# A graph network on one core: 448 late columns that carry their own row numbers, edge records loaded eight halves at a time, and one PSUM operand in each step of the sort

## The reference

```python
x = _layernorm(x + _L0_gnn_ref(x, edge_index, ...))   # mean of x[src] over dst, two matmuls, rows normalised
x = _layernorm(x + _L1_gnn_ref(x, edge_weight1, ...)) # one weight matrix per edge type, segment_sum over dst
x = _layernorm(x + _L2_gnn_ref(x, edge_index, ...))   # five rounds of: m = h @ W; agg = segment_sum(m[src], dst); GRU
x = _layernorm(x + _L3_gnn_ref(x, edge_index, ...))   # below
# _L3_gnn_ref, an MLP on every edge, summed over the edge's own source node:
row, col = edge_index[0], edge_index[1]
h = silu(concatenate([x[row], x[col], edge_attr]) @ eW1 + eb1)
m_ij = silu(h @ eW2 + eb2)
agg = segment_sum(m_ij, row)
update = silu(concatenate([x, agg]) @ nW1 + nb1) @ nW2 + nb2
```

## Time and profile before

| what | value |
|---|---|
| median of 3 runs | 10688.34 us |
| time of the profiled execution | 10691.69 us |
| its span in the profile | 10689.9 us, 154416 instructions |
| POOL busy | 8037.9 us (75%), 8249 instructions |
| PE, PEld busy | 6257.1 us (59%), 5701.5 us (53%) |
| DVE busy | 5456.2 us (51%) |
| ACT busy | 2205.1 us (21%) |
| first and last scatter of the sort start at | 75.8 and 1804.5 us |
| layer 0's gathers start at | 1815.5 us |
| layer 1's | 2933.7 us |
| layer 2's five rounds | 4044.8 us on |
| layer 3's | 9601.2 to 10652.7 us |

### The profile page before, as it was taken

The page is one execution under the profiler, slowest core; times in us unless marked ns, Lnnn a source line. Parts: engine busy times, 40 slices in busy tenths (PEclk is TensorE's granted clock), DMA queues, the critical chain, the costliest instruction groups (busy, mean ns, idle before and its releaser), DMA issues. The chain is left out here.

```text
span 10689.9 us, 154416 instructions
## 1 busy us (share of the span) xinstructions
PE 6257.1 (59%) x41996; PEld 5701.5 (53%) x41997; DVE 5456.2 (51%) x13690; ACT 2205.1 (21%) x6330; POOL 8037.9 (75%) x8249
## 2 busy tenths in 40 slices
PE   0000000555444436777677767776777688879998
PEld 0000000343333336777677767776777687878887
DVE  9993001444334434555455545554555466656666
ACT  1000000111133321111111111111111133336665
POOL 6777777777777777777777777777777777777776
PEclk9999999666655557888898878888989899989999
DMA  2000001222322233333433343334333433342223
GB/s 66 2 2 2 21 7 32 73 77 78 68 74 59 59 54 97 109 109 109 95 109 108 109 94 109 108 108 93 109 109 109 94 108 108 108 89 62 62 62 54
DMA packets 443301, 830.51 MB, mean 78 GB/s; under 512 B 179834, under 2 KB 260703, under 8 KB 442439
## 3 DMA queue, kind: packets, MB, share of 16 engines
q0 software_dynamic: 329728, 718.19, 26.8%
q1 hardware_dynamic: 113349, 109.89, 3.5%
HBM read 739.76 MB, written 87.77 MB: 77 GB/s over the span
## 5 line engine op out<-in xcount | busy, mean ns | idle before, releaser
L595 POOL DMA_INDIRECT rows<-state_table,rec x4160 | 4065.7, 977 | 1275.5 <-issue 1233.8
L666 DVE TENSOR_TENSOR agg<-agg,l_prod 128x250 f32 (+2 forms) x5824 | 2218.3, 381 | 3305.3 <-PE l_prod L643 1697.3
L643 PE MATMUL l_prod<-onehot,rows 128*128 128x125 f32 x16640 | 2538.4, 316 | 1234.3 <-DMA rows<-state_table,rec 656.9
L643 PEld LDWEIGHTS l_prod<-onehot,rows 128*128 128x128 f32 x16640 | 2359.8, 227 | 1377.3 <-DVE agg L666 1030.8
L640 PE MATMUL l_prod<-rows,onehot 128*125 128x130 f32 (+1 forms) x3328 | 758.8, 402 | 2100.4 <-DMA rows<-in_x_dram,rec 1569.0
L640 PEld LDWEIGHTS l_prod<-rows,onehot 128*125 128x125 f32 x3328 | 663.2, 296 | 2174.2 <-issue 1827.7
L294 POOL DMA_INDIRECT slots_table<-rec_stage,row_stage x784 | 809.4, 1032 | 305.8 <-issue 246.7
L649 DVE TENSOR_TENSOR onehot<-iota_row,rec 128x500 f32<-128x500 f32 x1465 | 987.1, 674 | 41.9 <-PEq L108 41.8
L1587 POOL DMA_INDIRECT l_gathered<-xcol_table,l_slots x832 | 799.2, 961 | 262.3 <-issue 253.0
L595 POOL DMA_INDIRECT rows<-in_x_dram,rec x832 | 800.0, 962 | 253.8 <-issue 250.2
L595 POOL DMA_INDIRECT rows<-rel_table,rec x832 | 793.4, 954 | 261.8 <-issue 228.6
(11 more groups left out here) (272 smaller groups left out, 8876.2 us busy)
## 6 DMA issues: line engine op xcount, KB each, us to landing
rows<-state_table,rec POOLq DMA_INDIRECT x4160
rel_table<-l_relrow SPq DMA_DIRECT2D x50, 500.0 KB
state_table<-l_row SPq DMA_DIRECT2D x200, 125.0 KB
slots_table<-rec_stage,row_stage POOLq DMA_INDIRECT x1312
rows<-in_x_dram,rec POOLq DMA_INDIRECT x832
rows<-rel_table,rec POOLq DMA_INDIRECT x832
l_gathered<-xcol_table,l_slots POOLq DMA_INDIRECT x832
slots_table<-fill SPq DMA_DIRECT2D x8, 936.0 KB
```

Source lines behind the costliest of these rows:

```text
L595: pool.indirect_dma_start(out=K["rows"][:, r, 0:width], out_offset=None, in_=table, in_offset=bass.IndirectOffsetOnAxis(ap=K["rec"][:, c, ...
L643: last = pe.matmul(p[:, s * SLOT:s * SLOT + LANES], K["rows"][:, r, s * D:(s + 1) * D], oh, start=True, stop=True)
L666: dve.tensor_tensor(into, into, of, ALU.add).then_inc(S.added, 1)
```

## The change

1. `LATE` is 448: the sort scatters 336 columns of key 1 in place of 528 (21 turns in place of 33), and the later phases scatter 66, 66, four times 66, and 52.
2. A late record has a 19th word, its row number (`REC_LATE`), in place of the separate `late_row`; the scatter takes its row number from the record.
3. `put_late` stands three turns before the end of the sort's scatters (`LAST_TURNS`).
4. In each step of the sort one operand lies in PSUM: the tile numbers (`tile_row`), the ones (`ones_c`), the running sums (`rank`) and the sum over five (`found`). The 128x2500 products stay as they were.
5. In layer 3 the records of eight halves, 288 KB, come with one DMA (`LOADED`), into one half of a ring of 16 (`DEEP`); gathered rows and one-hots keep 8 buffers (`FETCH`). The pipeline's loop unrolls 16 halves. SP's loop is written out.

```diff
-DEEP = 8
-FETCH = DEEP
+DEEP = 16
+FETCH = 8
+LOADED = 8
...
+REC_LATE = REC2 + 1
-LATE = 256
-LATE_LAYER, LATE_ROUND, LATE_LAST = 44, 34, 32
+LATE = 448
+LATE_LAYER, LATE_ROUND, LATE_LAST = 66, 66, 52
...
+        LAST_TURNS = 3
...
-        is_tile, rank = sb("is_tile", [L, FIVE, PART]), sb("rank", [L, FIVE, PART])
-        found, slot_i = sb("found", [L, PART]), sb("slot_i", [L, PART], I32)
+        is_tile, slot_i = sb("is_tile", [L, FIVE, PART]), sb("slot_i", [L, PART], I32)
-        ones_c = sb("ones_c", [L, PART])
...
+        rank = c.enter_context(nc.psum_tensor("rank", [128, 8, SLOT], F32))[0:L, 0:FIVE, 0:PART]
+        fixed = c.enter_context(nc.psum_tensor("fixed", [128, 4, SLOT], F32))
+        tile_row, ones_c, found = fixed[0:L, 0, :], fixed[0:L, 1, 0:PART], fixed[0:L, 2, 0:PART]
...
-                act.copy(K["late_row"][:], row[1][:, late]).then_inc(late_made, 1)
+                act.copy(late_all[:, :, REC2].bitcast(I32), row[1][:, late]).then_inc(late_made, 1)
...
-                for i in range(low, high):
-                    for h in range(2):
-                        stage(i, h, i + SC_TURNS, True)
-                if q == 1:
-                    put_late()
+                ends = [NOW_TURNS - LAST_TURNS, NOW_TURNS] if high == NOW_TURNS else [high]
+                for end in ends:
+                    for i in range(low, end):
+                        for h in range(2):
+                            stage(i, h, i + SC_TURNS, True)
+                    if end == NOW_TURNS - LAST_TURNS:
+                        put_late()
+                    low = end
...
+            step(dve.tensor_copy(tile_row, K["iota_row"][0:L, :]))
...
-                                               K["iota_row"][0:L, tiles][:, :, None].to_broadcast(part),
+                                               tile_row[:, tiles][:, :, None].to_broadcast(part),
...
-                out_offset=bass.IndirectOffsetOnAxis(ap=self.K["late_row"][:, self.at + c:self.at + c + 1], axis=0),
-                in_=self.K["late_rec"][:, c, :], in_offset=None).then_inc(self.done, 16)
+                out_offset=bass.IndirectOffsetOnAxis(ap=self.K["late_rec"][:, c, REC2:REC_LATE].bitcast(I32), axis=0),
+                in_=self.K["late_rec"][:, c, 0:REC2], in_offset=None).then_inc(self.done, 16)
...
+            def load(block):
+                area = block % (DEEP // LOADED)
+                if block >= DEEP // LOADED:
+                    sp.wait_ge(pre1_ok, block * LOADED - DEEP + LOADED)
+                sp.dma_start(slots[:, area * LOADED:(area + 1) * LOADED],
+                             table[:, block * LOADED * HALF:(block + 1) * LOADED * HALF, :]
+                             .rearrange("p (h k) w -> p h k w", k=HALF)).then_inc(slots_in[area], 16)
```

More of the change, by code:

```diff
@@ L385, in _ @@
             numbers = K["iota_row"][:, 0:TILES]
-            step(dve.memset(ones_c[:], 1.0))
+            step(dve.memset(ones_c, 1.0))
             dve.wait_ge(spares_made, 1)
@@ L605, in __init__ @@
         self.K, self.T, self.loaded, self.done = K, T, loaded, done
-        self.read, self.at = 0, 0
+        self.read = 0
     def load(self, sp, n):
@@ L612, in load @@
         sp.dma_start(self.K["late_rec"][:, 0:n, :].rearrange("p c w -> p (c w)"),
-                     self.T["late"][:, self.read * REC2:(self.read + n) * REC2]).then_inc(self.loaded, 16)
+                     self.T["late"][:, self.read * REC_LATE:(self.read + n) * REC_LATE]).then_inc(self.loaded, 16)
         self.read += n
@@ L1494, in edge_mlp @@
         loaded, zeroed = sem("loaded"), sem("zeroed")
-        slots_in = [sem(f"slots_in{q}") for q in range(DEEP)]
+        slots_in = [sem(f"slots_in{q}") for q in range(DEEP // LOADED)]
         onehot_ok = sem("onehot_ok")
@@ L1531, in _ @@
             STORE_LAG = NODE_LAG + 3
-            def load(i, off):
-                wait_half(sp, pre1_ok, i, off - DEEP)
-                sp.dma_start(slots[:, off % DEEP], table[:, bass.ds(number(i, off) * HALF, HALF), :])\
-                    .then_inc(slots_in[off % DEEP], 16)
+            def load(block):
[5 more added lines that the diff above has]
+                             .rearrange("p (h k) w -> p h k w", k=HALF)).then_inc(slots_in[area], 16)
             def store(k, buf):
@@ L1542, in store @@
                     .then_inc(stored[buf], 16)
-            def turn(i, off):
-                for q in range(DEEP):
-                    load(i, off + q)
-                    if q % 4 == 2:
-                        k = (off + q) // 4 - STORE_LAG
-                        if i is not None or k >= 0:
-                            store(k if i is None else i * (DEEP // 4) + k, k % 2)
             sp.wait_ge(late.done, 16 * LATE)
-            for j in range(DEEP):
-                load(None, j)
+            for block in range(DEEP // LOADED):
+                load(block)
             sp.wait_ge(zeroed, 1)
@@ L1568, in _ @@
             sp.dma_start(b2n[:], n_b2.rearrange("(a f) -> a f", a=1).to_broadcast([LANES, D])).then_inc(loaded, 16)
-            turn(None, DEEP)
-            turn(None, 2 * DEEP)
-            turn(None, 3 * DEEP)
-            with sp.Fori(4, HALVES // DEEP) as i:
-                turn(i, 0)
-            for k in range((HALVES // 4) - STORE_LAG, TILES):
+            for block in range(DEEP // LOADED, HALVES // LOADED):
+                load(block)
+                for k in range(block * LOADED // 4 - STORE_LAG, (block + 1) * LOADED // 4 - STORE_LAG):
+                    if k >= 0:
+                        store(k, k % 2)
+            for k in range(HALVES // 4 - STORE_LAG, TILES):
                 store(k, k % 2)
@@ L1582, in _ @@
                 q = half % FETCH
-                pool.wait_ge(slots_in[half % DEEP], half // DEEP * 16 + 16)
+                if half % LOADED == 0:
+                    pool.wait_ge(slots_in[half % DEEP // LOADED], half // DEEP * 16 + 16)
                 if half >= FETCH:
@@ L1732, in step @@
                     if i is not None:
-                        dve.wait_ge(stored[buf], i * 16 + (off // 4 - NODE_LAG - 1) // 2 * 16)
+                        dve.wait_ge(stored[buf], i * (DEEP // 8) * 16 + (off // 4 - NODE_LAG - 1) // 2 * 16)
                     elif k >= 2:
```

19 lines of the change are left out of this document (9 added, 10 removed).

## The result

The changed kernel takes 10655.5 us (median of 8 runs, 10651.35 to 10659.15), beside 10688.8 for the kernel before (8 runs, 10680.83 to 10698.51): ratio 0.997, 95% interval 0.996 to 0.9979. That is 33 us less, where the forecast was 42. The profiled execution took 10659.15 us, its span is 10657.4, 32.5 shorter than that of before.

The account below looks back on a forecast made before the run. The prediction took POOL's some 8200 indirect DMAs as the bound. Its terms, -44.7 + 2.5 - 2 + 1 + 0.9 = -42.3 us, took 10691.7 to 10649.4, by the median 10646; range 10632 to 10673.

Parts of the forecast that it names:

- Items 1 and 2: Sort steps: PSUM operands shorten first-key scatters, -44.7 us (bounds 0 and 58.6); DVE's own time +2.5 (0 to 10).
- the pointer operand of the earlier trace: Sort scans: pointer form took 349 ns with PSUM, 298 without; 50 scans by 0.05 us gave 2.5 us.
- Item 3: Sort and late groups: 192 scatters taken out save 245.0 us, put in cost 242.5; net -2 (-2.5 to +0.5).
- rival E: Phase tails: the moved scatters are free there, -242.5 us, 10404; chance 0.02.
- Item 4: Sort's end: the later, larger late table blocks scatters' landing; costs 3 us if caught, else 0; taken as +1.
- Item 5: Layer 3: POOL's first gather waits for 288 KB in place of 36, +0.9 us; later blocks are hidden.
- 8.5 us at a barrier: Barrier after a layer: listed among the small stretches left over besides POOL's DMAs; no change was forecast for it.
- B: Sort: an operand in PSUM frees nothing for a scatter; +2.4 us, 10691; chance 0.05.
- its half (scans): Sort: only the scans fail to free scatters, about 22 of the 44.7 us, 10668; chance 0.05.
- its "nothing": Sort: by the skill's rule that descriptor generation isn't contended, the PSUM operands would bring nothing; the prediction said the trace disagrees.
- C: First two sort parts: DVE slower with PSUM, 10 us before the first scatter, 10 before the 33rd; 10664; chance 0.06.
- D: Layer 3: POOL stops for blocks 24 times, 72 us at 3 us each, 10718; chance 0.06, including unnamed causes.

## Why the prediction was right, and by how much not

- **What bounds the kernel.** Right: every us of the change is on POOL, in the stretches named.
- **Items 1 and 2, the sort's operands.** Forecast -44.7 and +2.5, together -42.2; measured +0.9 and -43.3, together -42.4. The second key was to start at about 1090 and did at 1089.7, the mean was to be 975 and is 977. Part of this is luck: 2.5 us of DVE's own time were counted and 0.9 came. The six products keep 14.9 us with all else, where 13.9 were counted. DVE's share was 0.9 to the first scatter. Read over the two traces, the scan rose from 431 ns to 438 and the 128x560 comparison fell from 755 to 737: the pointer operand of the earlier trace rows, on which the 2.5 was built, has no part in it, and writing to PSUM costs 8 ns a reduction (1097 to 1105). Nor does the longer fixed cost of the Trainium skill ("VectorE: DVE Perf Modes", The TRN2 errata) show: as an estimate from its figures it came to 65 ns a step. The experiments show the operand as the cause scatter by scatter; the 42 us themselves only the first chip's two traces show.
- **Item 3, 192 scatters moved.** Forecast -2, measured -2.3. They are paid in full in the tails, as rows 6 had it (rival E is out).
- **Item 4, the late table.** Forecast +1, between 0 and 3; it is 0. ACT waited 3.4 us longer and the half ring covered it.
- **Item 5, layer 3's first block.** Forecast +0.9, measured 1.1 (from the drain's end to the first gather, 3.07 and 4.19 us).
- **The term that was missing.** The barriers were read once, as "8.5 us at a barrier", and taken as fixed. They are not: three of the four get 22, 22 and 20 more late scatters ahead of them (1.80, 1.80 and 1.63 us), and the sort ends 112 scatters behind a pause in place of 80 (2.51). That is 7.7 of the 9.8 us between 42.3 and 32.5. The rest is the 3.4 us over the gathers, which two executions can differ by, less about 1 us that item 4 didn't cost. It could have been read before: behind 44 late scatters the drain ends 6.93 us after the last, behind 32 it is 5.95.
- **The rivals.** B and its half (scans) are out on the first chip and in every timeline. So is the Trainium skill's inference ("SBUF — State Buffer", Who interferes with whom) that such instructions leave descriptor generation alone, as far as it is to hold for these DMAs. The prediction named both halves of the section and drew its "nothing" from this one alone. The other, that two inputs in SBUF contend with GpSimd's reads, agrees with the trace in so far as these DMAs have their row numbers in SBUF; that this is the reason no run here shows. C is out on the first chip; on the others a like thing happened by another way: DVE bounds the sort there, and with the PSUM operands the sort ends 20 to 42 us later. D is out on the first chip; on the others layer 3 loses 55 to 69 us (chip 10) and 19 to 28 (chip 4), by the profile at DVE's end of the loop. The prediction had not considered that the kernel might be bound elsewhere.

## What to carry to other kernels

Read every barrier of a phase, not one, and ask what it grows with: where two of them differ, the difference is a price per instruction that stands ahead of them. A stretch by another engine's operands is found by laying the stretched instructions against what ran beside them, and is cured by moving one operand. And a gain that rests on one engine being the bound holds only where it is; other conditions turned -33 us into +49, and the late columns, which with their drains cost 5 us on the first chip (-2.3 + 7.7), were the one of the three parts worth having there. And before a difference is put down to the chip, compare how complete the two traces are, as here by their counts of semaphore updates.

## What the runs showed of the hardware

- A POOL DMA begun under an instruction of DVE with two SBUF operands takes longer by what is left of that instruction: up to 3.42 us in place of 0.96 beside one of 2.76, and 0.96 beside the same instruction with one operand in PSUM.
- The drain of POOL's queue takes 0.082 us for each late scatter issued before it (32 to 66 of them, with 832 gathers ahead), landed or not; in the sort it counts from the last pause, and pauses come every 112 scatters. The 832 gathers of a phase show no such pauses.
- A DRAM write of 4256 KB took 12.9 us, and a load of 627 KB 4.8 (median of six), from issue to landing, and once a scatter landed 3.4 us late beside the first.
- The same program took 10.69 ms in one set of runs and 12.85 to 13.02 in others, with the same time for each instruction and each transfer and longer stops between the instructions of DVE and TensorE (one matmul every 2.80 us while POOL scatters). The traces of the slower runs lack about two thirds of the semaphore updates; chip and recording can't be told apart here.
